# Turning the queries before the window scores, and scaling them before the addition that ends a block, in a windowed-attention stack on one core

## What is computed

```
def attn_layer(x, Wqkv, qs, ksc, Wo):
    qkv = x @ Wqkv                                  # 128 -> 3 * 1024
    q, k, v = split and shape into 16 heads of 64
    q = l2norm(q) * qs ;  k = l2norm(k) * ksc
    q = q * cos * scale + rotate_half(q) * sin * scale
    k = k * cos * inv   + rotate_half(k) * sin * inv
    out = local_attention(q, k, v)                  # windows of 32; each looks at itself and the one before
    return out @ Wo

def ffn_layer(x, g, bln, W1, b1, W2, b2):
    xn = layernorm(x) * g + bln
    a, gate = split(xn @ W1 + b1)
    return a * gelu(gate) @ W2 + b2

for i in range(6):
    x = attn_layer(shift_tokens(x), ...) + x
    x = ffn_layer(shift_tokens(x), ...) + x
```

## Time and profile before

| | |
|---|---|
| median of three executions | 6553.5 us |
| the profiled execution, its own time | 6546.16 us |
| its span, from the first to the last instruction | 6544.4 us |
| TensorE busy | 5755.6 us (88%) |
| VectorE busy | 4565.4 us (70%) |
| GpSimd busy | 4279.6 us (65%) |
| ScalarE busy | 3404.7 us (52%) |
| granted TensorE clock, mean | 0.947 |

### The profile page before, as it was taken

How to read it: one execution, slowest core, us unless ns; L and a number is a source line. 1 busy time by engine, 2 the same in 40 slices (tenths; PEclk the granted TensorE clock), 3 DMA queues, 4 the chain that set the end, 5 groups by cost and what they waited for, 6 DMA issues and landing times. The chain is left out here.

```text
span 6544.4 us, 186553 instructions
## 1 busy us (share of the span) xinstructions
PE 5755.6 (88%) x76063; PEld 3951.0 (60%) x76063; DVE 4565.4 (70%) x6115; ACT 3404.7 (52%) x4021; POOL 4279.6 (65%) x2122
## 2 busy tenths in 40 slices
PE   6888887888888888889999999999688888888887
PEld 3444446666667666656555555554476666666665
DVE  4445427888888888856556556552588888888886
ACT  1234355666666666623444444434466666666664
POOL 1000008878887888715777777778788878788884
PEclk6789898999999999989999999999899999999999
DMA  0000002222222222200000000000122222222221
GB/s 24 1 1 2 2 16 63 70 67 74 63 70 64 68 64 67 62 12 1 1 1 1 1 1 1 1 1 1 50 61 74 64 68 64 68 67 67 59 68 47
DMA packets 188334, 254.69 MB, mean 39 GB/s; under 512 B 60828, under 2 KB 81816, under 8 KB 187288
## 3 DMA queue, kind: packets, MB, share of 16 engines
q1 hardware_dynamic: 187416, 242.03, 14.2%
HBM read 38.98 MB, written 1.57 MB: 6 GB/s over the span
## 5 line engine op out<-in xcount | busy, mean ns | idle before, releaser
L2075 POOL TENSOR_TENSOR XB<-XB,Pb 128x1024 f32<-128x1024 f32 x448 | 1070.4, 2389 | 338.3 <-ACT Pb L2035 297.5
L908 POOL TENSOR_TENSOR sin_qk<-raw_qk,rot 128x512 f32<-128x512 f32 x768 | 998.3, 1321 | 87.4 <-ACT raw_qk L816 53.7
L2085 DVE TENSOR_REDUCE b_pmax<-slot 128x1 f32<-128x512 f32 x1024 | 653.5, 683 | 325.0 <-PE slot L1822 323.9
L2035 ACT ACTIVATE Pb<-slot 128x1024 f32<-128x1024 f32 x512 | 502.6, 1024 | 702.2 <-PE slot L1933 649.4
L924 POOL TENSOR_TENSOR rot_out<-rot_out,sin_qk 128x1024 f32<-128x1024 f32 x192 | 605.3, 3153 | 392.0 <-DVE rot_out L982 391.1
L941 POOL TENSOR_TENSOR inv_norm<-norm2c,minus_half 128x16 f32<-128x16 f32 x192 | 665.9, 3468 | 169.1 <-DVE norm2c L1083 168.6
L530 PE MATMUL slot<-w_hi,x_hi 128*128 128x512 f32 x1152 | 544.6, 473 | 70.2 <-POOL w_lo L899 46.8
L781 ACT ACTIVATE qT<-slot 128x1024 f32<-128x1024 f32 x192 | 197.2, 1027 | 739.9 <-PE slot L537 739.9
L937 POOL TENSOR_TENSOR inv_norm<-norm2c,minus_half 128x16 f32<-128x16 f32 x192 | 559.2, 2913 | 0.0
L706 PE MATMUL slot<-kT,qT 64*32 64x64 f32 x24576 | 336.7, 231 | 215.8 <-issue 215.6
L1513 DVE TENSOR_REDUCE part_max<-slot 128x1 f32<-128x512 f32 (+3 forms) x640 | 360.7, 605 | 237.4 <-PE slot L1316 123.2
(11 more groups left out here) (213 smaller groups left out, 13253.2 us busy)
## 6 DMA issues: line engine op xcount, KB each, us to landing
VW<-V SPq DMA_DIRECT2D x1152, 128.0 KB
VW<-V SPq DMA_DIRECT2D x768, 64.0 KB
w_raw<-in_Wqkv SPq DMA_DIRECT2D x36, 512.0 KB, 3.7
Wo<-in_Wo SPq DMA_DIRECT2D x12, 512.0 KB, 4.2
W<-in_W SPq DMA_DIRECT2D x12, 341.0 KB, 3.3
consts<-in_shape_constants SPq DMA_DIRECT2D x1, 2436.5 KB, 8.9
QH<-rows_dram SPq DMA_DIRECT2D x128, 2.0 KB
QB<-rows_dram SPq DMA_DIRECT2D x128, 2.0 KB
```

The source lines that it names most:

```text
L908: ins = pool.tensor_tensor(dst[:, :, x, :], src[:, :, 1 - x, :], tab, ALU.mult)
L2035: act.activation(Pb[:, at % B_RING, :], slot[n % 2][:, :], ACT.Exp).then_inc(s["b_exp"], 1)
L2075: pool.tensor_tensor(b_sum[:, window % 2, :], Pb[:, (at - 1) % B_RING, :] if k == 1 else b_sum[:, window % 2, :], Pb[:, at % B_RING, :], A ...
L2085: dve.tensor_reduce(b_pmax[:, n // 2, u:u + 1], o[:, 512 * x:512 * x + 512], AX.X, ALU.max)\
```

## The change

Two pieces of the step are written at another place. On TensorE the turn of the queries of chunk k-1 comes before the scores of chunk k-2, right behind the value products, with its waits. On VectorE the scaling of the queries, and behind it the third tile of `hide`, come before the addition `XA`. Nothing is added, nothing is taken away, and no size or buffer changes.

```
--- before.py
+++ after.py
@@ -679,6 +679,12 @@  (TensorE, step)
                     mm.then_inc(s["pv_mm"], 1)
 
+                c = at.chunk(1)
+                if c is not None:
+                    pe.wait_ge(s["qn_done"], START + g + c + 1)
+                    wait_for_slot2()
+                    turn(slot[2], rot_out[0]).then_inc(s["tq_mm"], 1)
+
                 c = at.chunk(2)
                 if c is not None:
                     pe.wait_ge(s["qT_sb"], START + g + c + 1)
@@ -711,12 +717,6 @@
                 c = at.chunk(1)
                 if c is not None:
-                    pe.wait_ge(s["qn_done"], START + g + c + 1)
-                    wait_for_slot2()
-                    turn(slot[2], rot_out[0]).then_inc(s["tq_mm"], 1)
-
-                c = at.chunk(1)
-                if c is not None:
                     if c == 0:
                         pe.wait_ge(s["w_lo_done"], START + third_of(call, layer, 3))
@@ -1102,6 +1102,16 @@  (VectorE, step)
+                c = at.chunk(2)
+                if c is not None:
+                    dve.wait_ge(s["rq_done"], START + g + c + 1)
+                    dve.wait_ge(s["iq_done"], START + g + c + 1)
+                    normalise(0, "qn_done")
+
+                b = at.block(10)
+                if b is not None:
+                    hide(layer, f, b, 2)
+
                 b = at.block(11)
                 if b is not None:
                     if b % NB == 0:
@@ -1112,16 +1122,6 @@
                                                  in1=XB[p, cols], op0=ALU.add, op1=ALU.add).then_inc(s["f_done"], 1)
-
-                c = at.chunk(2)
-                if c is not None:
-                    dve.wait_ge(s["rq_done"], START + g + c + 1)
-                    dve.wait_ge(s["iq_done"], START + g + c + 1)
-                    normalise(0, "qn_done")
-
-                b = at.block(10)
-                if b is not None:
-                    hide(layer, f, b, 2)
```

## The result

The changed kernel takes 6663.59 us (median of 4 runs, 6656.18 to 6671.89), the kernel before in the same comparison 6548.57 us (4 runs). The ratio is 1.0173, with a 95% interval of 1.0146 to 1.0200: slower by 115 us, where 24 us faster was forecast, and outside the range that was given. The profiled execution has a span of 6654.4 us, 110 us above the one before.

A forecast was written before the change was run, and what follows sets the result against it. VectorE waits for scores, and these for the fetch of TensorE's code. Terms of -21 (waits), -17 (cosines) and +14 us (late code) sum to -24 us from 6546.16, 6522, put down as 6525; range 6465 to 6590.

The forecast's parts named there:

- its place relative to the maximum unchanged: GpSimd's sine half and norms were to keep their timing relative to VectorE's maximum; no cost was put down.
- VectorE's own work: VectorE over one block of four steps: 72.55 us less 5.47 us of real waits, 67.08 us.
- VectorE's new waits: VectorE before the maximum, four steps: 0.65, 1.83, 0.65 and 1.90, sum 5.03 us a block against 5.47 before.
- The way from the scaling to the maximum: From scaled queries over turn, mask and scores to VectorE's maximum: 4.30, 4.98, 4.81 and about 4.50 us by step.
- The semaphores between scaling and turn: Delay from VectorE's scaling to TensorE's turn, taken as 0.15 us between bounds of 0.05 and 0.44 us.
- step 1: Step of four with the rotary tables: way 4.30 us against VectorE's own 3.65 us, new wait 0.65 us.
- the code's arrival: Fetch of TensorE's code for the scores, to pass during the 0.84 us turn; 0.3 us a block, 14 us, taken off.
- step 2: Step of four with the third hide: way 4.98 us against VectorE's own 3.15 us, new wait 1.83 us.
- The gap inside the scores: TensorE's idle time put down to "issue" was to fall from 73.2 us to under 20 in 64 chunks.
- The two signs set down for a miss on the slow side: A gap inside the scores staying over 50 us, or growth of the exponential's 14.9 us wait, in 64 chunks.
- The wait for the scaled queries becomes the pace: Rival at the turn in the first two steps: 1.82 us of waits stay, 1.38 us a block lost, 6595 us; chance 0.15.
- The gap is no fetch or does not shrink: Rival on TensorE: the turn adds in full to the way to the maximum, 1.14 us a chunk, 6727 us; chance 0.04.

The follow-up runs named there:

- e3: Changed kernel with the clamp of the query norms put later, behind the reciprocal of the sums; ratio 1.0039 of the kernel before.
- e6: Changed kernel without the clamp of the query norms, the power reading the sum of squares itself; ratio 1.0013 of the kernel before.
- e7: Changed kernel with the late clamp, and the mask's two products with all waits of the scores ahead of the turn; ratio 0.9995 of the kernel before.
- e8: Changed kernel with the late clamp, turn ahead of the scores only in the step with XA and the one after it; ratio 0.9951, 6529.5 us.
- e2: Kernel before with VectorE's half of the change only (scaling and third hide ahead of XA); ratio 0.9995.
- e1: Kernel before with TensorE's half of the change only (turn ahead of the scores); ratio 1.0238.
- e4: Kernel before with the clamp of the query norms put later, behind the reciprocal of the sums; ratio 0.9988.
- e5: Kernel before with the clamp of the query norms put behind the cosines of the keys; ratio 1.0014.
- e9: Kernel before with a second clamp of the query norms, into its own tile, ahead of the real one; ratio 1.0019.
- e10: Changed kernel with the late clamp and six more mask products ahead of the turn in the step with the rotary tables; ratio 1.0003 of the kernel before.

## Why the prediction was wrong

**The step that failed** is the one on GpSimd: "GpSimd, which adds the sine half and makes the norms, has its place relative to the maximum unchanged", and with it that VectorE's own work stays 67.08 us a block, with no term for instructions that become longer. The clamps of the query norms alone grew by 130 us, 2.7 us a block. The sine half for the keys waits for ScalarE's copy, and the copy follows the key projection, which the change brings 0.84 us nearer to the maximum; the same prediction counts on that for VectorE's waits. In 1200 to 2400 us GpSimd waited 20.1 us for this copy before and waits 0.3 us after. That put the sine half 0.20 us ahead of the clamp where it had been 0.08 us behind it. The row that warned of it was there: line 1030 with 433 ns in the mean, where an undisturbed one takes 0.17 us. Its price is by e3 about 1.3 points of 1.7, and e6, without the clamp, agrees.

**The size of VectorE's new waits** was the second. 5.03 us a block were forecast, 241 us in 48 blocks; measured are 401.2, or 8.4 a block, and 118.9 in 1200 to 2400 us, where 70 to 85 were forecast. The way from the scaling to the maximum was priced too short in every step (the means above add up to 22.3 us a block, the forecast's to 18.6). Three of its terms were too small. The semaphores between scaling and turn were taken as 0.15 us and are 0.32 in the mean of step 1. The turn, mask and scores were priced at the full clock in steps in which TensorE had waited for up to 3 us just before (6.41 us in the slow step shown). And the code's arrival was taken as covered by the turn in step 2, where 0.95 us stayed open in the step shown. e3 is 27 us above the kernel before where the forecast is 24 below it; e7 takes 29 us of that away by a shorter way.

**What held.** The gap inside the scores falls where the turn stands ahead: 73.2 to 20.4 us in 1200 to 2400, about as forecast (under 20), and 55.2 in e8, where it is ahead in two steps of four. In the whole execution TensorE's gaps put down to "issue" fall from 311.0 to 136.3 us and do not just move elsewhere. That fits the fetch of code; no run changes the fetch alone. The 175 us so freed on TensorE did not shorten the time, as VectorE set it. The waits at the cosines (71.3 to 19.3) and at the exponential (50.5 to 6.4) went. `XA` behind the scaling costs nothing, by e2, and is worth 0.65 points once the turn is ahead, by e1. The two signs set down for a miss on the slow side, a gap inside the scores over 50 us and a longer wait for the exponential, did not come, although the miss did: neither looks at how long VectorE's own instructions take.

**The rivals.** "The wait for the scaled queries becomes the pace" named the right side and the right place, and its 49 us of loss are of the order of e3's 27, but by another way: the 1.82 us in step 1 on which it rested did go in the changed kernel (in the mean of step 1 the two waits are 1.15 us before and 0.03 after). "The gap is no fetch or does not shrink" is out as far as the gap shrank. None of them had the clamp.

## What to carry to other kernels

When work on one engine is brought forward, list also what the third and fourth engines start because of it, and lay their starts beside the short instructions of the engine that sets the pace; a group whose mean is well above its shortest one (here 433 against 174 ns) can already be showing such a collision. A piece put in front of another engine's work is cheap only in steps in which its own engine is the later one: here the same move gained about 0.4% in two steps of four (e8 against e4), and with it in all four the kernel was 0.4% slower than before even with the clamp moved (e3).

## What the runs showed of the hardware

- A `tensor_scalar` of 16 columns in SBUF on VectorE takes 0.17 us alone and 1.11 us if it begins 0.2 us into a GpSimd multiplication of 1.27 us that reads and writes SBUF; begun 0.1 to 0.6 us into one it took 0.71 to 1.21 us, and in both kernels it ended 0.03 to 0.04 us after that instruction. Begun 1.2 us into it, it is short (e5). GpSimd's power on 16 columns (2.9 to 3.9 us) had no such effect: in the kernel before 99 clamps of the key norms begin under it, and all are short.
- The same multiplication went with a longer `tensor_tensor` of 128 columns with two inputs in SBUF (`x_lo`, line 1129): 43 begun under it in the kernel before took 1.34 to 1.37 us, the 145 begun under the power 0.27 to 0.29 us.
- 140 us of longer clamps cost 0.2% where VectorE had waits to spare (e9); in the changed kernel, taking 174 us of clamp time away gained 1.3% (e3).
- After 2.60 us without a product TensorE's granted clock was 0.50 for the next 3.4 us and more; with six products in the wait, so that 1.52 us of it were empty, it stayed 1.00 (e10, the step shown).
